# Four GNN layers on one core: joint statistics, relus on VectorE, one bank for the message sum, a new order

## What is computed

```python
    h = jnp.maximum(_layernorm(x, axis=-1), 0.0)
    x = x + _L0_gnn_ref(h, adj, L0_gnn_W, L0_gnn_a)   # attention with leaky relu, 128 columns, and h W itself
    h = jnp.maximum(_layernorm(x, axis=-1), 0.0)
    x = x + _L1_gnn_ref(h, adj, L1_gnn_W, L1_gnn_b)   # deg * (h Wi + b) + A (h Wj): the message layer
    h = jnp.maximum(_layernorm(x, axis=-1), 0.0)
    x = x + _L2_gnn_ref(h, adj, ...)                  # 8 heads of 32, masked softmax, projection
    h = jnp.maximum(_layernorm(x, axis=-1), 0.0)
    x = x + _L3_gnn_ref(h, adj, L3_gnn_W, L3_gnn_a_src, L3_gnn_a_dst)   # attention, 256 columns
```

## Time and profile before

| | us |
|---|---|
| median of 3 runs | 1141.49 |
| lowest, highest | 1141.29, 1145.17 |
| profiled execution, span | 1144.0 |

### The profile page before, as it was taken

How to read it: one execution, slowest core, us unless ns; L and a number is a source line. 1 busy time by engine, 2 the same in 40 slices (tenths; PEclk the granted TensorE clock), 3 DMA queues, 4 the chain that set the end, 5 groups by cost and what they waited for, 6 DMA issues and landing times.

```text
span 1144.0 us, 38802 instructions
## 1 busy us (share of the span) xinstructions
PE 1054.0 (92%) x14872; PEld 883.0 (77%) x14872; DVE 1043.0 (91%) x2911; ACT 1056.3 (92%) x3145; POOL 949.6 (83%) x1734
## 2 busy tenths in 40 slices
PE   4689999999999999999999999999999999999964
PEld 3467888788878878887887888888888888888752
DVE  4489999999999999999999999999999999999961
ACT  3489999999999999999999999999999999999862
POOL 3888899889989989988898988889888988998521
PEclk9899999999999999999999999999999999999997
DMA  5369999999999999999999999999999999999872
GB/s 149 68 110 167 180 177 182 167 187 171 181 176 178 171 169 182 180 179 168 182 167 179 183 178 173 169 189 171 174 176 183 170 168 190 180 174 156 151 139 51
DMA packets 643514, 190.05 MB, mean 166 GB/s; under 512 B 607232, under 2 KB 643328, under 8 KB 643328
## 3 DMA queue, kind: packets, MB, share of 16 engines
q1 hardware_dynamic: 642560, 187.24, 94.9%
q10 hardware_dynamic: 768, 0.33, 0.1%
HBM read 19.73 MB, written 16.78 MB: 32 GB/s over the span
## 4 chain that ended last, share of the span: by engine, by line
ACT 47%; DMA 16%; POOL 14%; PE 12%; DVE 9%; issue 3%; POOLq 0%; SPq 0%; DVEq 0%
DMA h_t<-h_rows 11%; PE ps L403 3%; DMA mix_t<-mix_rows 3%; PE ps L405 3%; PE ps L404 3%; ACT ps L1053 3%; ACT ps L1042 3%; ACT ps L1048 3%; ACT ps L1059 3%; POOL h_rows L1189 3%; POOL h_rows L1249 2%; ACT relu L973 2%; ACT relu L964 2%; ACT query_hi L1030 2%; ACT key_hi L1033 2%
## 5 line engine op out<-in xcount | busy, mean ns | idle before, releaser
L403 PE MATMUL ps<-w_hi,h_t 128*128 128x256 f16 (+2 forms) x1280 | 330.5, 265 | 31.4 <-DMA h_t<-h_rows 28.3
L404 PE MATMUL ps<-w_lo,h_t 128*128 128x256 f16 (+2 forms) x1280 | 329.5, 264 | 0.0
L405 PE MATMUL ps<-w_hi,h_t 128*128 128x256 f16 (+2 forms) x1280 | 326.4, 264 | 0.0
L403 PEld LDWEIGHTS ps<-w_hi,h_t 128*128 128x128 f16 x1280 | 125.3, 98 | 53.7 <-DMA h_t<-h_rows 33.0
L403 PE MATMUL ps<-h_t,w_hi 128*128 128x256 f16 x512 | 139.6, 273 | 0.0
L405 PE MATMUL ps<-h_t,w_lo 128*128 128x256 f16 x512 | 139.6, 273 | 0.0
L404 PE MATMUL ps<-h_t,w_hi 128*128 128x256 f16 x512 | 139.6, 273 | 0.0
L405 PEld LDWEIGHTS ps<-w_hi,h_t 128*128 128x128 f16 x1280 | 125.6, 98 | 14.3
L404 PEld LDWEIGHTS ps<-w_lo,h_t 128*128 128x128 f16 x1280 | 126.3, 99 | 13.2
L1185 POOL TENSOR_SCALAR h_rows<-relu 128x512 f16<-128x512 f32 x64 | 39.5, 618 | 64.3 <-ACT relu L964 64.3
L403 PEld LDWEIGHTS ps<-v_hi,head_t_hi 128*128 128x128 f16 x1024 | 79.9, 96 | 8.8 <-issue 2.3
(11 more groups left out here) (181 smaller groups left out, 4622.4 us busy)
## 6 DMA issues: line engine op xcount, KB each, us to landing
x<-in_x SPq DMA_DIRECT2D x64, 256.0 KB, 3.9
out<-x SPq DMA_DIRECT2D x64, 256.0 KB, 2.7
h_t<-h_rows SPq DMA_TRANSPOSE x256, 3.6
head_t_hi<-head_hi SPq DMA_TRANSPOSE x64, 4.7
head_t_lo<-head_lo SPq DMA_TRANSPOSE x64, 6.2
mix_t<-mix_rows SPq DMA_TRANSPOSE x64, 3.4
w_f<-in_w_o SPq DMA_DIRECT2D x1, 256.0 KB, 4.1
w3t_f<-in_w_t SPq DMA_DIRECT2D x1, 256.0 KB, 3.8
```

The lines of the kernel that those rows point to most:

```text
L403: pe.matmul(o, lh, rh, start=start, stop=False)
L404: pe.matmul(o, lh, rl, start=False, stop=False)
L405: return pe.matmul(o, ll, rh, start=False, stop=stop)
```

## The change

- **Joint statistics.** One bn_stats over 512 elements, in which the two graphs' elements alternate, replaces two over 256. It gives a mean and a sum of squares for each of the two, so the aggregates go. In the statistics tile (3 values a graph) column 1 is the mean, column 2 the sum of squares.
- **Small steps.** `add_epsk` moves from GpSimd to VectorE. `negate_meank` goes; `shift1` and `shift2` are one instruction each on VectorE; layers 0 and 3 have none.
- **Relu of the outer layers on VectorE.** For layers 0 and 3 it is max(x - mean, 0) from SBUF to SBUF. Their scale rstd is put on later, where ScalarE evicts the features (`keep_feat0_b`, now two instructions, and `keep_feat3_b`), times 1/256, by way of DEFER_VAR and DEFER_EPS.
- **Message layer in one bank.** The message source is divided by the degree (kept above 1), the aggregate's matrix is scaled by 256, and `gather` goes on summing in `mi_ps`. One VectorE instruction adds the whole. Statistics of layer 1 stay with ScalarE's relu.
- **Mixed heads.** `head_norm_b` writes a float32 tile `mix_f`; GpSimd casts and subtracts it (`rows_hi_mix`, `rows_lo_mix`), 128x512 each.
- **Order and banks.** Every engine's list is in a new order with other parts, PARTS is 9 (73 slots), and all banks are given out anew. Matmuls, transfers and their sizes are the same.

```diff
-PARTS = 7
+PARTS = 9
...
-        ag_ps = ps[3]
...
             def gather(g):
                 pe.wait_ge(split_message_done, g + 1)
-                pe.matmul(ag_ps[:, :], agg[:, :], mj_hi[g % 2][:, :], start=True, stop=False)
-                last = pe.matmul(ag_ps[:, :], agg[:, :], mj_lo[g % 2][:, :], start=False, stop=True)
+                pe.matmul(mi_ps[:, :], agg[:, :], mj_hi[g % 2][:, :], start=False, stop=False)
+                pe.matmul(mi_ps[:, :], agg[:, :], mj_lo[g % 2][:, :], start=False, stop=True).then_inc(gather_done, 1)
...
-            def mean_var0(g):
-                dve.wait_ge(stats0_0_done, g + 1)
-                dve.bn_aggr(moments0[g % 2][:, 0, :], stats0[g % 2][:, 0, :])
...
+            def both_stats0(g):
+                dve.bn_stats(stats0[g % 2][:, :, :].rearrange("p b s -> p (b s)"), x[g % XBUF][:, :, :].rearrange("p b d -> p d b")).then_inc(both_stats0_done, 1)
...
+            def add_eps0(g):
+                dve.tensor_scalar(vareps0[g % 2][:, :], stats0[g % 2][:, :, 2], DEFER_VAR, DEFER_EPS, ALU.mult, ALU.add).then_inc(add_eps0_done, 1)
...
+            def norm0_0(g):
+                dve.tensor_scalar(relu0[g % 2][:, 0, :], x[g % XBUF][:, 0, :], stats0[g % 2][:, 0, 1:2], 0.0, ALU.subtract, ALU.max).then_inc(norm0_0_done, 1)
+
+            def norm0_1(g):
+                dve.wait_ge(both_stats0_done, g + 1)
+                if g >= 2:
+                    dve.wait_ge(rows_lo0_done, g - 1)
...
+            def shift1(g):
+                dve.wait_ge(power1_done, g + 1)
+                dve.scalar_tensor_tensor(nshift1[g % 2][:, :], stats1[g % 2][:, :, 1], -1.0, rstd1[g % 2][:, :], ALU.mult, ALU.mult).then_inc(shift1_done, 1)
...
+                act.activation(g0[g % 2][:, 1, 1:1 + F0W], f0_ps[:, 1 * F0W:2 * F0W], ACT.Copy, scale=rstd0[g % 2][:, 1:2])
...
+            def rows_hi_mix(g):
+                pool.wait_ge(head_norm_0_done, g + 1)
+                pool.tensor_scalar(mix_rows[g % 2][:, 0, :, :], mix_f[g % 2][:, :, :], 1.0, 0.0, ALU.mult, ALU.add).then_inc(rows_hi_mix_done, 1)
...
```

More of the change, by code:

```diff
@@ L152, in build @@
         ps = [ctx.enter_context(nc.psum_tensor(f"ps{k}", [P, BANK], F32)) for k in range(BANKS)]
[L153 to L158, removed]
-        ag_ps = ps[3]
-        q_ps = ps[1]
-        k_ps = ps[2]
-        v_ps = ps[0]
[L163 to L167, removed]
+        f0_ps = ps[1]
+        r0_ps = ps[1]
+        p0_ps = ps[3]
+        s0_ps = ps[1]
+        mj_ps = ps[3]
+        mi_ps = ps[7]
+        q_ps = ps[3]
+        k_ps = ps[7]
+        v_ps = ps[0]
+        sc0_ps = ps[6]
+        sc1_ps = ps[2]
+        sc2_ps = ps[4]
+        sc3_ps = ps[5]
+        sh0_ps = ps[3]
         sh1_ps = ps[1]
[L169 to L172, removed]
+        pr_ps = ps[1]
+        f30_ps = ps[6]
+        f31_ps = ps[4]
+        r3_ps = ps[7]
         p3_ps = ps[0]
-        s3_ps = ps[0]
+        s3_ps = ps[5]
         sc_ps = [sc0_ps, sc1_ps, sc2_ps, sc3_ps]
@@ L394, in _ @@
         def _(pe):
-            def turn(bank, src, b):
-                for c in range(KC):
-                    last = pe.transpose(bank[:, (c * GROUP + b) * P:(c * GROUP + b + 1) * P], src[:, b, c * P:(c + 1) * P], ident[:, :])
-                return last
             def triple(o, lh, ll, rh, rl, start, stop):
@@ L580, in project_0, with project_1 @@
                     pe.wait_ge(w_split, W_TURN.index("o") + 1)
+                for c in range(KC):
+                    last = triple(pr_ps[:, 0 * D:1 * D], mix_t[g % 2][:, 0 * KC + c, :], mix_t[g % 2][:, (GROUP + 0) * KC + c, :], w_hi[:, c, COL_WO:COL_WO + D], w_lo[:, c, COL_WO:COL_WO + D],
+                                  start=(c == 0), stop=(c == KC - 1))
+                last.then_inc(project_0_done, 1)
+            def project_1(g):
+                if g == 0:
+                    pe.wait_ge(w_split, W_TURN.index("o") + 1)
                 pe.wait_ge(move_out_done[g % 2], 16 * (g // 2) + 16)
@@ new lines, in slot @@
+                at(9, row_max3)
+                at(8, norm3_1)
+                at(6, head_max_3)
+                at(3, inv_sum0)
+                at(8, norm3_0)
+                at(3, update0_0)
+                at(3, update0_1)
+                at(6, head_max_0)
+                at(3, both_stats1)
+                at(9, inv_sum3)
+                at(3, add_eps1)
+                at(4, split_message)
+                at(6, head_max_2)
+                at(7, invert_heads_1)
+                at(3, shift1)
@@ new lines, in slot @@
+                at(7, head_norm_1)
+                at(7, invert_heads_0)
+                at(7, head_norm_0)
+                at(0, both_stats0)
+                at(6, head_max_1)
+                at(6, split_head_3)
+                at(4, update1)
+                at(8, add_eps3)
+                at(6, split_head_0)
+                at(4, both_stats2)
+                at(0, norm0_1)
+                at(1, add_eps0)
+                at(6, split_head_2)
+                at(9, update3_0)
+                at(4, add_eps2)
@@ L947, in _ @@
+                at(0, norm0_0)
+                at(6, split_head_1)
+                at(9, update3_1)
+                at(2, row_max0)
             run(slot)
@@ L1274, in slot @@
             def slot(at):
[L1275 to L1301 removed]
+                at(9, rows_hi3)
+                at(4, power1)
+                at(2, rows_hi0)
+                at(9, rows_lo3)
+                at(8, rows_hi_mix)
+                at(4, rows_hi1)
+                at(8, rows_lo_mix)
+                at(4, rows_lo1)
+                at(7, add_out_bias)
+                at(5, power2)
+                at(9, power3)
+                at(2, rows_lo0)
+                at(3, add_feat0)
+                at(5, rows_hi2)
+                at(5, rows_lo2)
+                at(4, add_deg_bias)
+                at(2, power0)
             run(slot)
```

596 lines of the change are left out of this document (233 added, 363 removed).

## The result

| | before | changed |
|---|---|---|
| median, us | 1143.33 (4 runs) | 1222.88 (4 runs) |
| lowest, highest | 1141.29, 1145.53 | 1222.72, 1225.18 |
| profiled span | 1144.0 | 1223.4 |

The changed kernel is slower: ratio 1.0703, 95% interval 1.0682 to 1.0724. The forecast was 1245, with a range of 1108 to 1305; the forecast of slower holds, its size was 102 us where 79.6 were measured.

A forecast was written before the change was run, and what follows sets the result against it. VectorE was to bound, held by GpSimd at 18.0 us a group, where ScalarE was fullest at 16.45: 1144.0 + 64 x (18.0 - 16.45) + 4 = 1247, less 2.5: 1245 us, range 1108 to 1305.

The forecast's parts named there:

- The bound and the period before: Kernel before, steady stretch: ScalarE fullest, 0.24 us idle a period; 40 groups in 658 us, 16.45 us each.
- VectorE without meetings: VectorE's work a group if it never waits for GpSimd: 15.92 - 4.47 + 3.90 = 15.35 us.
- The meetings: VectorE's SBUF-only instructions wait until GpSimd's running instruction ends: nine waits of 0.28 us, 2.5 us a group.
- other waits: VectorE's waits on anything but GpSimd: 0.15 us a group, less than ScalarE's 0.24.
- Sum of the two: VectorE's period a group: 15.35 of work plus 2.5 of waits on GpSimd, 17.85, with 0.15 more, 18.0 us.
- Fill and drain: Start and end of the run, 73 slots for 71: 4 us more, bounds 0 and 12.
- B: VectorE against GpSimd: only the relus wait, or waits are short; period 16.6, 1155 us (1140 to 1190); chance 0.15.
- C: The ten VectorE instructions fall where GpSimd doesn't hold them; TensorE bounds at 15.9; 1110 us (1095 to 1128); chance 0.25.
- D: VectorE's joint statistics take two steps an element, 2.1 us more a group: 1219 us, or 1379 with GpSimd waits; chance 0.08.
- E: New order waits for itself, at bank 7 and `shift1` after `add_eps1`: 0.5 us a group, 1150 to 1180 us; chance 0.05.
- The signs named for the changed profile: Relus near 0.6 us mean, maximum above 1; GpSimd subtracts above 1163 ns; VectorE fullest, 97% or more; period 18.0 us.
- the sign of being wrong: Forecast wrong if VectorE's eps and relu rows show one tight duration, or if TensorE has the fullest queue.

The follow-up runs named there:

- experiment 6: Changed kernel with layer 0's second relu, its eps and layer 3's two relus moved, layer 1's power earlier, layer 2's shift on GpSimd: 1169.9 us.
- experiment 1: Changed kernel with layer 0's second relu and the eps behind it moved in VectorE's list to where GpSimd is idle: 1183.6 us.
- experiment 2: Changed kernel with GpSimd's 128x512 add of the output bias cut into two of 128x256: 1223.8 us.
- experiment 4: Changed kernel with the four relus of layers 0 and 3 on ScalarE and two negated means on GpSimd: 1191.6 us.
- experiment 5: Changed kernel with the four relus on ScalarE, layer 0's eps moved to where GpSimd is idle, layer 2's shift on GpSimd: 1157.2 us.
- e6: Kernel of experiment 6 with layer 3's eps also moved to where GpSimd is idle and GpSimd's subtract for layer 3 earlier: 1170.2 us.

## Why the forecast was right in kind and 22 us too high

By its own steps:

- **The bound and the period before.** The order of engines held. The period did not: 658 us do not hold 40 groups, but 39.7, at 16.58 us. Of the 22 us, 64 x 0.13 = 8 come from here. Every figure "a group" of that part is short by 0.8%.
- **VectorE without meetings,** 15.35 forecast. Measured 17.90 - 2.0 = 15.9. The miscount gives 0.12. The statistics step by 0.61, not 0.60 (0.06 for four). Layer 1's eps takes its two constants from tiles and steps by 0.195, not 0.07; the message's rest, with a pointer operand for a constant, by 0.66 for 0.575. Together 0.39, which with the 0.15 put down for other waits is the difference. The relus were sized right (0.262 for 0.27).
- **The meetings,** 2.5 forecast, 2.0 measured. The rule was right for adds, casts and subtracts: wait for the end of GpSimd's instruction, less the start. It was wrong for the four powers, which were counted among the holders (1.96 of the 14.3) and in experiment 6 held no relu; without them the same estimate gives 0.25 us for 0.28. The kinds were right too, both one-input forms and two-input ones, wide or of two elements. The number was off: nine were taken to meet at random, but a fixed order has no chance in it. The same three relus and one shift met in each group, four of ten. Of the other six, `add_eps1`, `add_eps2` and the relu behind it stand where GpSimd waits for just these eps, `add_eps0` stands behind a held relu, at whose end GpSimd is idle, and `add_eps3` and `shift1` at the change between two GpSimd instructions; I had seen the first alone. In return one of the four cost 0.93, three times the mean.
- **Sum of the two:** 18.0 forecast, 17.90 measured. Two errors, 0.4 too little work (15.5 with the other waits, for 15.9) and 0.5 too much for the meetings, nearly cancel. That the period is right to 0.1 is luck, and so in part is the price of the meetings, four at 0.5 us where nine at 0.28 were counted. The mechanism is not.
- **Fill and drain,** +4 forecast: 79.4 us more span less 64 x 1.32 = 84.5 is -5. The first groups of the changed kernel start 12.3 to 17.2 us apart (L779) and don't pay the steady price. These 9, the 8 above and 64 x 0.1 = 6 for the period make the 24 us by which the span was missed (1247 for 1223.4). The 22 of the median are 2 less, since its median lies 0.5 us under its profiled span, not 2.5.
- **ScalarE** was put at 14.2 (13.7 to 14.8) and has 14.9, just outside; **GpSimd** at 14.2, or 15 to 15.5 held, and has 14.6. Neither bounds.
- **Rivals.** B (1155: only the relus wait) failed by its price, since the relus alone cost 1.65 us, not 1.1, and by its kind, since the small ones wait as well (experiments 1, 2 and 4). C (1110: no waits, TensorE bounds) was given 0.25. The waits did not fall under its 0.9. And where most of them were taken away, the time came to 1157 (experiment 5, the relus on ScalarE) and 1170 (experiment 6), not 1110. In e6 the waits that are left come to 0.25 us a group, well under C's 0.9, so C's condition is met there and its bound, TensorE, is not what follows. D is excluded by the statistics' 0.69 to 0.71 us. E is no cause at 17.90, since VectorE idles 0.08 us a group there. What stands next is of its sort, a chain of the new order, but through SyncE's list and not through bank 7 or `shift1`.
- **How much the meetings explain.** Of the 79.6 us, one relu moved gave back 39 (experiment 1), and the moves of experiment 6 gave back 53. The other 27, or more, stand in every version that keeps the relus on VectorE; the chain through SyncE's queue is the reading for them, and it is not shown.
- **The signs named for the changed profile** came in the main: relus with a maximum over 1 us, VectorE the fullest (94% of the span for the 97 named, 99.6% in the steady stretch). The relus' mean is 0.75 for 0.6, and the three plain eps (L716, L789, L864) show one tight duration in the steady stretch, where they meet nothing, which is half of what the forecast had named as the sign of being wrong. GpSimd's subtracts grew to at most 1213 ns; the loser was nearly always VectorE, since a relu of 0.27 holds GpSimd for little (its add L1154 took 1.32 for 1.27).

## What to carry to other kernels

Before work is moved to VectorE in a form that reads and writes SBUF alone, look at what GpSimd runs at that moment in its list: for a cast, subtract or add the price is the rest of that instruction, nearly the same in every turn of a fixed order, and a neighbour of the same kind inherits it when only one instruction is moved. Put such instructions where GpSimd waits for VectorE anyway, all of them together, and count the small ones. When the engine that was full is freed, follow the chain through the queues of transfers before expecting the next engine's length as the new period.

## What the runs showed of the hardware that was not expected

- A one-input instruction of two elements, alone on the engine 0.15 us, took 1.22 us behind GpSimd's add (experiment 4), and 0.69 behind half of it (experiment 2). The Trainium skill ("Vector Engine (DVE) Microarchitecture Reference", 5.1) has two elements of one input in SBUF in the two-port mode; these rows agree.
- Not every form waits, and not every GpSimd instruction holds. Two relus ran in 0.33 and 0.35 us inside a GpSimd power, which took 0.83 for 0.70 (experiment 6). A reciprocal of two elements from SBUF to SBUF took 0.15 us inside a GpSimd cast with 0.55 left (experiment 5).
- A difference of 0.05 us decides. An eps at the change between two GpSimd instructions took 0.16 us in most groups and up to 1.17 in others of the same run, which turned a period of 17.07 into 17.9 there.
- A statistic whose elements lie 1 KB apart in turn ran at the full rate: 0.61 us from start to start for 512 elements, 0.33 for 256 in a row. The Trainium skill (same page, 5.2) has a figure for hopping (1.73 ns a column) and an exception for one stream alternating between two regions; the exception holds here.
